# Two prefetch counts of an edge gather are raised: 57 instead of 42 before the first aggregation, 36 instead of 20 before the second

## The reference

```python
xn = _layernorm(x, axis=-1)
x = x + _L0_gnn_ref(xn, sent_repr, src, dst, ...) + _L0_mix_ref(xn[None], ...)[0]
x = x + _L0_ffn_ref(_layernorm(x, axis=-1)[None], ...)[0]
xn = _layernorm(x, axis=-1)
x = x + _L1_gnn_ref(xn, edge_index, edge_weight, ...) + _L1_mix_ref(xn[None], ...)[0]
x = x + _L1_ffn_ref(_layernorm(x, axis=-1)[None], ...)[0]
```

## Time and profile before

| | us |
|---|---|
| median of 3 executions | 2210.39 |
| the three executions | 2210.05, 2210.39, 2223.58 |
| span of the profiled execution, first to last instruction | 2177.7 |
| busy: PE, DVE, POOL, ACT | 1591.3, 1251.5, 1067.5, 862.1 |
| 440 gathers of the first layer on POOL | 430.1 |
| 416 gathers of the second layer on POOL | 405.6 |

### The profile page before, as it was taken

How to read it: one execution, slowest core, us unless ns; L and a number is a source line. 1 busy time by engine, 2 the same in 40 slices (tenths; PEclk the granted TensorE clock), 3 DMA queues, 4 the chain that set the end, 5 groups by cost and what they waited for, 6 DMA issues and landing times. The chain is left out here.

```text
span 2177.7 us, 31463 instructions
## 1 busy us (share of the span) xinstructions
PE 1591.3 (73%) x7770; PEld 1251.9 (57%) x7770; DVE 1251.5 (57%) x3879; ACT 862.1 (40%) x2965; POOL 1067.5 (49%) x1173
## 2 busy tenths in 40 slices
PE   5635577766756786969999766877788887875892
PEld 4533444444444455959999654655566655664792
DVE  3523555555556687855777635454455455676435
ACT  2221656656555786635777431000011000143451
POOL 3751666666666500421222156666666666326351
PEclk8755668667777898989999867888888888896896
DMA  6741544444444302836555133333333333122786
GB/s 193 223 138 40 150 121 126 127 131 126 123 123 142 108 18 84 260 111 203 180 171 179 62 89 106 90 93 91 88 91 88 92 90 93 52 93 85 219 264 223
DMA packets 176882, 276.92 MB, mean 127 GB/s; under 512 B 28920, under 2 KB 132218, under 8 KB 176456
## 3 DMA queue, kind: packets, MB, share of 16 engines
q0 software_dynamic: 50352, 136.58, 21.8%
q1 hardware_dynamic: 82194, 94.23, 14.2%
q10 hardware_dynamic: 44166, 44.14, 6.1%
HBM read 202.35 MB, written 73.58 MB: 127 GB/s over the span
## 5 line engine op out<-in xcount | busy, mean ns | idle before, releaser
L501 POOL DMA_INDIRECT ring<-feat_d,src_lane x440 | 430.1, 977 | 281.8 <-issue 120.8
L1221 POOL DMA_INDIRECT rows<-xn_d,src_of x416 | 405.6, 975 | 228.7 <-issue 108.6
L1201 PE MATMUL bank<-ring,a_hot 128*128 128x260 f32 x880 | 318.9, 514 | 139.7 <-DVE ring L1100 81.4
L1392 PE MATMUL bank<-rows,big 128*128 x880 | 286.5, 443 | 129.1 <-DVE big L1300 68.9
L1130 ACT ACTIVATE ring<-ring 128x64 f32<-128x64 f32 x1540 | 375.3, 336 | 6.3 <-issue 5.6
L1201 PEld LDWEIGHTS bank<-ring,a_hot 128*128 128x128 f32 x880 | 207.5, 253 | 213.6 <-DVE ring L1100 95.7
L1309 DVE TENSOR_TENSOR big<-bank,big 128x256 f32 x440 | 186.7, 424 | 222.0 <-DMA m_bo<-in_L_mix_bo 114.7
L1392 PEld LDWEIGHTS bank<-rows,big 128*128 128x128 f32 x880 | 164.7, 209 | 225.9 <-issue 211.1
L1085 DVE TENSOR_TENSOR acc<-bank,acc 128x260 f32 x440 | 187.1, 425 | 143.2 <-DMA m_dst_bc<-dst_lo_d 60.9
L1362 ACT ACTIVATE big<-bank,a_col 128x256 f32<-128x256 f32 (+1 forms) x26 | 13.1, 552 | 416.9 <-PE bank L1407 177.5
L1300 DVE TENSOR_SCALAR big<-const,dst_lane,ew_lane 128x128 f32<-128x128 f32 x440 | 155.3, 353 | 1.0 <-PEq L95 1.0
(11 more groups left out here) (405 smaller groups left out, 2893.6 us busy)
## 6 DMA issues: line engine op xcount, KB each, us to landing
slots_d<-fold ACTq DMA_DIRECT2D x25, 1300.0 KB, 5.7
e_w_now<-in_L_ffn_w SPq DMA_DIRECT2D x56, 256.0 KB
a_dst_bc<-dst_lo_d SPq DMA_DIRECT2D x23, 512.0 KB
big<-in_L_ffn_W SPq DMA_DIRECT2D x16, 512.0 KB
e_x<-slots_d SPq DMA_DIRECT2D x56, 130.0 KB
ring<-feat_d,src_lane POOLq DMA_INDIRECT x440
rows<-xn_d,src_of POOLq DMA_INDIRECT x416
e_ys<-y_d SPq DMA_DIRECT2D x24, 256.0 KB
```

Of the source, the lines that this page charges most:

```text
L501: pool.indirect_dma_start(ring[:, q % RING, at, :], None, table, bass.IndirectOffsetOnAxis(ap=src_lane[:, n:n + 1], axis=0)).then_inc(gath ...
L1201: pe.matmul(bank[n % BANKS][:, 0:D + H], hot[:, q % HOTS, at, :], ring[:, q % RING, at, :], start=True, stop=True)\
L1221: pool.indirect_dma_start(rows[:, n % RING1, :], None, table, bass.IndirectOffsetOnAxis(ap=src_of[:, n:n + 1], axis=0)).then_inc(gathered[ ...
L1392: pe.matmul(bank[n % 4][:, 0:D], hot[:, n % HOTS, :], tile_of(rows, slots[n % 4]), start=True, stop=True)\
```

## The change

The two numbers are raised. The first mixer's stage then issues gathers 39 to 95 (57) and the first aggregation 96 to 439; the second mixer's stage issues 0 to 35 (36) and the second aggregation 36 to 415. The conditions of the waits, the rings and all other engines' instructions stay as they are.

```diff
-BY_THEN = EARLY[NI + 1] + 42
+BY_THEN = EARLY[NI + 1] + 57
...
-PREFILL = 20
+PREFILL = 36
```

## The result

The changed kernel took 2245.16 us (median of 4 runs, 2236.61 to 2256.95) against 2211.8 us (4 runs) for the kernel before on the same chip: ratio 1.0148, 95% interval 1.0111 to 1.0184, or 32.7 us slower (24.6 to 40.7). The forecast was 2231 us; its range ended at 2242.

What follows compares the result with a forecast made beforehand. The prediction took PE, held up by long unbroken runs of gathers, to bound the mixers and aggregation starts. Terms 17.3 - 4.6 + 16.2 - 8.0 = +20.9 us on 2210.39 gave 2231.3 us, 0.95% slower; range 2213 to 2242.

Steps and rivals of the forecast that it cites:

- What bounds the mixers: Both mixers' stages: PE's results come late in long unbroken runs of gathers, so PE, not POOL, sets their length.
- First mixer +17.3: First mixer's stage: 15 more gathers take 18.8 us, about one tile gets done meanwhile, so +17.3 us.
- First aggregation -4.6: Start of the first aggregation: 15 fewer gathers let the copy after PE's mixer product start earlier, -4.6 us.
- Second mixer +16.2: Second mixer's stage: 16 more gathers take 20.1 us, three tiles get through beside them at 6.0 us each, +16.2 us.
- the stated upper bound: Second mixer's stage: no tile gets through beside the 16 further gathers, +20.1 us.
- Second aggregation -8.0: Start of the second aggregation: 16 fewer gathers spare PE its early hold-up, -8.0 us, bounds -5.6 and -11.5.
- The 32.7 us between span and median: Whole kernel: the 32.7 us between profiled span 2177.7 and median 2210.39 us were left as they are.
- The memset: Second mixer: the 3.90 us memset holds up the gathers and PE recovers, +7.7 instead of +16.2, 2222.8 us; chance 0.18.
- Nothing is given back: Aggregations' starts: their pauses only move, so the mixers' +33.5 us stays whole, 2243.9 us; chance 0.12.
- something else: Mixers: PE is held up by another cause, such as code fetch; only +3.8 us remains, 2214.2 us; chance 0.09.
- Faster, the gather is paid wherever it is issued: Aggregations: each gather issued there costs 1.50 us, so they lose 22.5 and 24.0, total -13.0, 2197.4 us; chance 0.09.

Runs made afterwards that it cites:

- e7_plain: Kernel before with 8 first-mixer gathers instead of 42, plus 40 plain transfers of the same size from SP's queue; +9.3 us (2.2 to 16.4).
- e12_pool_plain: Kernel before with 8 first-mixer gathers instead of 42, then 34 plain transfers in GpSimd's own queue; one run, 2191.77 against 2191.94 us.
- e1_base_again: The kernel before, measured and profiled once more with no edit; 2226.86 us, ratio 1.000 (0.9971 to 1.003).
- e2_first_only: Kernel before with only the first number raised, 57 gathers instead of 42 in the first mixer; ratio 1.0054 (1.0025 to 1.0082).
- e8_thin: Kernel before with 15 further gathers of 16 bytes a row after the first mixer's 42; +23.5 us (16.8 to 29.9).
- e11_both_again: The changed kernel once more, 57 and 36 gathers, against the kernel before; 2245.25 us, ratio 1.013 (1.0073 to 1.0186).
- e4_few: Kernel before with fewer gathers in both mixers, 8 instead of 42 and 10 instead of 20; ratio 1.0032 (0.9999 to 1.0066).

## Why the prediction was wrong, step by step

Mechanism and sign were right, the size was too small: by the pieces +27.8 in place of +20.9, and by the times +32.7, whose interval starts at 24.6. Of the 6.9 us between forecast and pieces, 4.2 lie in the second mixer and 2.1 in the second aggregation.

- *What bounds the mixers* (PE held up in long unbroken runs of gathers, not GpSimd): right, and shown by taking the gathers away (-43.1), making them thin (no difference), replacing them (54.1, 54.7 us) and pausing (63.5 us). The rule of the Trainium skill, page "SBUF — State Buffer", section "Who interferes with whom", that PE and ACT wait for nobody, was no guide here. PE's own next instruction does start at once (193.79 above), but PE's results reach their readers some 25 us late (190.45 above) beside GpSimd's indirect transfers, and PE then waits for these readers. The rule's other half, that transfers don't contend with a compute engine, agrees with e7_plain and e12_pool_plain.
- *First mixer +17.3:* measured 113.3, 112.2 and 113.7 less 95.6, mean +17.5. The number is right, in part by luck, as two errors offset each other: the usual pace was back 9 us after the last gather (198.99 to 208.05), not 5, but two tiles, not one, were done in the longer hold-up (copies of 190.45 and 202.41).
- *First aggregation -4.6:* the copy of L1135 lost its 4.6 us as read, and the gain at chunk 48 is 4.5, 3.4 and 2.9. Right, or 1 us too large.
- *Second mixer +16.2:* **this term failed.** Measured 68.4, 68.7 and 67.2 less 48.0, mean +20.1. I took a tile every 6.0 us, three tiles, beside the further gathers, from the last two intervals before their end. But the hold-up deepens with the length of the run (6.4, 11.2, 14.0 us): beside the 16 further gathers one tile got through in each trace (1324.45 above), and the next came 2.6 to 4.1 us after them. So the stage came out at the number of the stated upper bound. The first mixer's trace had shown it: the 19.6 us for a tile there are the mean of 9.8 and 29.4 us (142.91, 152.73 in the row below, 182.12). Nor was 6.0 us typical of the second mixer: with the same 20 gathers e1_base_again, e2_first_only and e8_thin have 9.9, 9.2 and 8.5 us between the last copy beside them and the first behind their end.
- *Second aggregation -8.0:* mis-sized too. The gain of 8.8 us at step 16 is there, between the two values read from the rows (5.6 and 11.5), and the next unbroken run of gathers takes part of it back: 6.4 at step 32, 5.9, 5.8 and 6.8 at step 48. The miss of 1.8 us is no more than single traces scatter here (2.4).
- *The 32.7 us between span and median,* which I carried along as if they lay outside the kernel: wrong, though without effect on the difference. The changed kernel's profiled execution has a span of 2241.7 and a time of 2243.28, 1.6 us outside. The profiled execution of before was simply some 30 us faster than the timed ones.

The first mixer's trace of before, ACT's copy between those of 142.91 and 182.12:

```profile
152.73 0.28 ACT L821 ACTIVATE m_ek<-bank 128x128 f32<-128x128 f32 x1 [6.72 <-issue]
```

In the means of the three traces the mixers make +37.6 and the starts -9.8; the forecast had +33.5 and -12.6. The remaining 4.9 us from 27.8 to the measured 32.7 are within the interval; no run shows a place for them.

*The rivals.* The memset does not hold GpSimd. In the trace above they didn't meet, but in e11_both_again, the same kernel, the 3.90 us memset starts at 1310.72 amid the gathers, and those of 1310.80, 1312.06 and 1313.31 take 0.95 us each and stay 1.25 apart. "Nothing is given back" is nearest by number (2243.9). The starts of both aggregations do gain, but only as far as chunk or step 48 is that shown: the change was timed at +32.7 and +28.8, and both intervals take in the mixers' +37.6 alone; "something else" is refuted by e4_few's mixers. "Faster, the gather is paid wherever it is issued" had half of the truth: with more gathers at the aggregations' starts each costs 1.45 us there, with fewer nothing like it comes back, because the 15 that went are those that cost 0.3 us each. The pieces' sum, +27.8, would have been 2238.2 and within the range; what carried the median past its end at 2242 is the 4.9 us that no piece shows, and the 1.4 us by which that chip's runs of before lay above the ones I started from. The range had no room for the scatter of the executions, which on one chip went from 2210.88 to 2238.94 us for the kernel before (31 executions).

## What to carry to other kernels

When one engine's stretch is slow beside a background stream of another engine, don't ask only how much of the stream fits in; ask what the stream costs per piece in an unbroken run and after a pause. Here 34 further gathers in one run cost 43 us in the mixer and 32 in groups of eight 11, and moving them elsewhere without pauses only moved the price. When extrapolating a stall, use the value at the depth that the change reaches, not the last interval seen.

## What was unexpected of the hardware

- GpSimd's indirect transfers hold up the delivery of TensorE's results, from some 10 us into an unbroken run: with 8 gathers the fourth and fifth tile of the first mixer are copied 11.7 and 13.0 us after the run's start, with 42 gathers 18.3 and 28.1 us after it; 15 with 16 bytes a row add as much as 15 with 1040 (113.4 and 113.3 us for the stage), while 34 to 40 plain transfers of 1040 bytes a row, from SP's or GpSimd's queue, add 1.6 and 2.2 us to 52.5.
- The first late result comes 2 to 6 us after the last gather; in the first mixer the usual pace is back 5 to 7 us after it with 42 gathers and 9 with 57. Pauses of 4 to 6 us after each eight gathers keep the hold-up away almost wholly.
- ACT's and DVE's updates reach PE at once in the meantime (0.15 us from DVE's L767 to PE's L839 at 193.79): in these rows only PE's own updates are late.
- All traces and times were taken with the same recording of the execution, so whether the recording has a part in the hold-up stays open.
